# Adapter norm moved into a scan chain, split q/k/v projections, and paired max jobs in a four-layer conditioned sequence kernel

## The reference

```python
# layer 0: state-space layer with a complex scan, then an MLP 256 -> 1024 -> 256
y = y + gate_a * s5(ln(y) * (1 + scale_a) + shift_a)
y = y + gate_ff * (gelu(mod(ln(y)) @ W1 + b1) @ W2 + b2)
# layer 1: one-head attention over 1024 tokens, width 256
h = film(rmsnorm(x, norm1_w), cond, film1_w, film1_b)
Q = h @ q_w + q_b
K = h @ k_w + k_b
V = h @ v_w + v_b
attn = softmax(Q K^T * 256 ** -0.5)
x = x + ((attn @ V) @ proj_w + proj_b)
x = x + gelu(film(rmsnorm(x, norm2_w), ...) @ mlp_w1 + mlp_b1) @ mlp_w2 + mlp_b2
# layer 2: rank-8 adapter whose four maps are made from the conditioning row
h = gelu(layernorm(ada_emb, ln_g, ln_b) @ W1 + b1)
w = h @ W2 + b2
# layer 3: 16-head attention (head width 16) over 1024 tokens
energy = q k^T
att = softmax(energy) / 256 ** 0.5
```

## Time and profile before

| what | value |
|---|---|
| median of three runs | 879.32 us (878.69 to 881.57) |
| the profiled execution, its own time | 880.76 us |
| its span | 878.9 us |
| mean granted TensorE clock | 0.982 |
| PE busy | 838.7 us, 95% of the span |
| DVE busy | 666.1 us, 76% |
| ACT busy | 459.4 us, 52% |
| POOL busy | 227.3 us, 26% |

### The profile page before, as it was taken

The page is one execution under the profiler, slowest core; times in us unless marked ns, Lnnn a source line. Parts: engine busy times, 40 slices in busy tenths (PEclk is TensorE's granted clock), DMA queues, the critical chain, the costliest instruction groups (busy, mean ns, idle before and its releaser), DMA issues.

```text
span 878.9 us, 13287 instructions
## 1 busy us (share of the span) xinstructions
PE 838.7 (95%) x4978; PEld 521.8 (59%) x4978; DVE 666.1 (76%) x1139; ACT 459.4 (52%) x840; POOL 227.3 (26%) x377
## 2 busy tenths in 40 slices
PE   6999999999999999999989989999999999999994
PEld 3668888958977998887845433333333333333342
DVE  8998657676538577646458879999999999999377
ACT  4646232144332443333232158888878878888760
POOL 4443412202002103112112710233333333333411
PEclk9999999999999999999989969999999999999998
DMA  8613122110000000000597600505050505000002
GB/s 314 252 49 97 55 92 98 49 52 2 1 1 1 1 1 1 2 1 1 168 182 193 252 1 3 92 21 92 21 93 21 92 21 93 23 27 24 27 25 73
DMA packets 29379, 57.40 MB, mean 65 GB/s; under 512 B 7228, under 2 KB 15152, under 8 KB 29314
## 3 DMA queue, kind: packets, MB, share of 16 engines
q1 hardware_dynamic: 22596, 44.40, 19.2%
q0 software_dynamic: 6720, 12.15, 4.7%
HBM read 39.26 MB, written 14.91 MB: 62 GB/s over the span
## 4 chain that ended last, share of the span: by engine, by line
PE 83%; DVE 8%; ACT 5%; POOL 2%; issue 2%; DMA 0%; DVEq 0%; ACTq 0%; POOLq 0%
PE PA L1531 15%; PE PA L1542 15%; PE PD L1327 10%; PE PA L1305 8%; PE PA L1253 7%; PE PD L1502 7%; PE PA L1408 5%; PE PD L1378 4%; PE PA L1246 2%; PE PA L1398 1%; PE PD L1600 1%; DVE NMX L2045 1%; PE PA L1477 1%; ACT R L1107 1%; PE PD L1253 1%
## 5 line engine op out<-in xcount | busy, mean ns | idle before, releaser
L2045 DVE TENSOR_REDUCE NMX<-PD 128x2 f32<-128x1024 f32 x256 | 301.9, 1220 | 25.7 <-PE PD L1502 21.2
L1107 ACT ACTIVATE R<-PA 128x512 f32<-128x512 f32 x512 | 267.0, 603 | 71.6 <-PE PA L1531 69.8
L1531 PE MATMUL PA<-STKR 50*128 50x512 f32 x512 | 185.3, 454 | 3.6 <-ACT R L1107 2.5
L1531 PEld LDWEIGHTS PA<-STKR 50*128 50x128 f32 x512 | 83.2, 188 | 151.7 <-ACT R L1107 139.3
L1502 PE MATMUL PD<-STKR 48*128 48x512 f32 x512 | 150.0, 456 | 4.2 <-DVE NMX L2045 4.1
L1043 ACT ACTIVATE R<-PA,VEC 128x512 f32<-128x512 f32 x64 | 43.8, 687 | 104.1 <-PE PA L1305 91.6
L1327 PE MATMUL PD<-WHR,HSR 128*128 128x256 f32 x512 | 95.3, 285 | 0.5 <-DVE HSR L1918 0.5
L1327 PEld LDWEIGHTS PD<-WHR,HSR 128*128 128x128 f32 x512 | 82.1, 191 | 6.1 <-issue 2.0
L1305 PE MATMUL PA<-XSR,WHR 128*128 128x512 f32 x256 | 81.2, 398 | 3.9 <-issue 2.0
L1502 PEld LDWEIGHTS PD<-STKR 48*128 48x128 f32 x512 | 62.0, 188 | 30.1 <-DVE NMX L2045 13.4
L1327 PE MATMUL PD<-WLR,HSR 128*128 128x256 f32 x256 | 72.4, 283 | 0.0
(11 more groups left out here) (288 smaller groups left out, 1181.3 us busy)
## 6 DMA issues: line engine op xcount, KB each, us to landing
STKR<-qk_terms SPq DMA_DIRECT2D x32, 384.0 KB, 8.8
R<-in_l_w SPq DMA_DIRECT2D x8, 1024.0 KB, 5.0
W<-in_w SPq DMA_DIRECT2D x4, 1024.0 KB, 10.7
qk_terms<-PARTS SPq DMA_DIRECT2D x8, 512.0 KB, 3.4
qk_terms<-PARTS POOLq DMA_DIRECT2D x8, 512.0 KB, 3.8
S<-row_reciprocals POOLq DMA_DIRECT2D x56, 64.0 KB, 2.1
X<-in_x SPq DMA_DIRECT2D x4, 512.0 KB, 8.5
qk_terms<-PARTS SPq DMA_DIRECT2D x8, 256.0 KB, 5.0
```

The lines of the kernel that those rows point to most:

```text
L1107: act.activation(PB[:, n % 2, j, :], PA[:, e % NEB, :], ACT.Exp).then_inc(s_exp3, 1)
L1531: pe.matmul(PA[:, e % NEB, :], KS[rows, slot(gg), jj, kt * P:(kt + 1) * P], QS[rows, slot(gg), jj, c * HALF:(c + 1) * HALF], start=True, s ...
L2045: ve.tensor_reduce(out, PD[:, o:o + NROW, :], axis=AX_X, op=ALU.max, negate=True).then_inc(s_mred, 1)
```

## The change

Three edits of one file. (1) `ada_normalise` is called from `bu` of the second part, between the scan and the product with C2; the stage `an` is gone and `gc` moves ahead of `ad 0`. (2) The q, k and v projections of layer 1 use fp32r halves and three products: DVE splits the q and k weights in a new stage `wh`, the v weight in `wv`, and every XT tile in the DVE part of `n1`; the halves of the tiles lie where the MLP's halves lay (XSR), those of the weights in C2, S2 and in the place of WA. The stage `n1 0` moves three down jobs ahead, into the MLP. The last statistics and the norm of batch 1 leave the end of the MLP and run on DVE inside batch 0's attention, as jobs `hs` and `hn` behind the first and the second score of the loop. (3) In the 8 `qk3` jobs of batch 1 three max jobs come in twos; three fewer stand alone ahead of the first step, and the turn `tm` comes later by two max jobs.

```diff
-         ("an", 0), ("nn", 1), ("ya", 0), ("n0", 1), ("ad", 0), ("gc", 0), ("cg", 1), ("y0", 0), ("yn", 0), ("ad", 1), ("bu", 2),
+         ("nn", 1), ("ya", 0), ("n0", 1), ("gc", 0), ("ad", 0), ("cg", 1), ("y0", 0), ("yn", 0), ("ad", 1), ("bu", 2),
...
-             {NTILE - 1: [("h0", 0)], B * NTILE - 6: [("wt", 0)], B * NTILE - 4: [("wv", 0)]})
+             {NTILE - 1: [("h0", 0)], B * NTILE - 6: [("wt", 0)], B * NTILE - 5: [("wh", 0)], B * NTILE - 4: [("wv", 0)],
+              B * NTILE - 3: [("n1", 0)]})
...
-SCHED += weave([("qk3", QJOBS + j) for j in range(QJOBS - 1)], [("mx", EARLY + j) for j in range(QJOBS - 1)])
-EARLY += QJOBS - 1
-assert UNIT == EARLY
-SCHED += [("qk3", 2 * QJOBS - 1), ("mx", EARLY), ("tm", 0)]
-SCHED += weave([("v3", TWO + j) for j in range(TWO)], [("mx", EARLY + 1 + j) for j in range(TWO)])
-SCHED += [("mx", n) for n in range(EARLY + 1 + TWO, LEAD)]
+for j in range(QJOBS):
+    SCHED += [("qk3", QJOBS + j), ("mx", EARLY)]
+    EARLY += 1
+    if EARLY >= UNIT + 2 and ("tm", 0) not in SCHED:
+        SCHED.append(("tm", 0))
+    elif j % 2 and j < QJOBS - 1:
+        SCHED.append(("mx", EARLY))
+        EARLY += 1
...
+            jobs += [(("hs", "hn")[t], 0)] if t < 2 else []
...
             def qk(b):
+                pe.wait_ge(s_whalf, 2)
+                terms = [(k, w, x) for k in range(KB) for w, x in TERMS]
+                for name, weights in zip("qk", WQKV):
                     for c in range(NC):
-                        xt_ready(b, "n1", c)
+                        pe.wait_ge(s_half1, (b * NC + c + 1) * KB)
                         for k in range(KB):
-                            project(abank(b, name, c, k), WA[:, w], k * P, b, c, s_afull)
+                            o = abank(b, name, c, k)
+                            for n, (i, w, x) in enumerate(terms):
+                                m = pe.matmul(o, weights[w][:, i, k * P:(k + 1) * P],
+                                              XTR[:, (1 - b, b)[x], i, c * HALF:(c + 1) * HALF],
+                                              start=(n == 0), stop=(n == len(terms) - 1))
+                            m.then_inc(s_afull, 1)
...
+                if part == 1:
+                    ada_normalise(0)
                 ve.wait_ge(s_z, part + 1)
                 ve.tensor_tensor(ZC[:, q], Z[:, q], C2[:, q], ALU.mult).then_inc(s_zc, 1)
...
-                    if t % TPC == TPC - 1:
+                    if t % TPC == TPC - 1 and (b, h) != (B - 1, NC - 1):
                         stats(b, lambda h: None, [h])
...
+            def weight_halves(_):
+                ve.wait_ge(s_wain, 32)
+                for w in range(2):
+                    high, low = WQKV[w]
+                    link(ve.tensor_copy(high, WA[:, w]))
+                    ve.tensor_tensor(low, WA[:, w], high.bitcast(F32), ALU.subtract).then_inc(s_whalf, 1)
+
+            def tile_halves(b):
+                for _, tag, h, k in turned(b, "n1"):
+                    evacuated(ve, b, tag, h, k)
+                    high, low = (XTR[:, x, k, h * HALF:(h + 1) * HALF] for x in (1 - b, b))
+                    tile = XT[:, b, k, h * HALF:(h + 1) * HALF]
+                    link(ve.tensor_copy(high, tile))
+                    ve.tensor_tensor(low, tile, high.bitcast(F32), ALU.subtract).then_inc(s_half1, 1)
```

More of the change, by code:

```diff
@@ L133 @@
 SOLO = turn_step(NUNIT - 1) + 1
-SCHED += weave([("qk3", QJOBS + j) for j in range(QJOBS - 1)], [("mx", EARLY + j) for j in range(QJOBS - 1)])
-EARLY += QJOBS - 1
-assert UNIT == EARLY
-SCHED += [("qk3", 2 * QJOBS - 1), ("mx", EARLY), ("tm", 0)]
-SCHED += weave([("v3", TWO + j) for j in range(TWO)], [("mx", EARLY + 1 + j) for j in range(TWO)])
-SCHED += [("mx", n) for n in range(EARLY + 1 + TWO, LEAD)]
+for j in range(QJOBS):
[6 more added lines that the diff above has]
+        EARLY += 1
+assert ("tm", 0) in SCHED
+SCHED += weave([("v3", TWO + j) for j in range(TWO)], [("mx", EARLY + j) for j in range(TWO)])
+SCHED += [("mx", n) for n in range(EARLY + TWO, LEAD)]
 AFTER = {SOLO + 2 * j + i: [(("p3a", "p3")[i], j)] for j in range(TWO - 1) for i in range(2)}
@@ L193, in act_jobs @@
         for kind, x in attention(stage):
-            jobs += {"s": [], "v": [(b, "v1", x)], "t": [(b, "p", x, i) for i in range(2)], "o": [(b, "o", x)]}[kind]
+            jobs += {"s": [], "v": [(b, "v1", x)], "t": [(b, "p", x, i) for i in range(2)], "o": [(b, "o", x)]}.get(kind, [])
         return jobs
@@ L302, in build @@
             PARTS = [at(f"PARTS{u}", o, [P, 2, 2, HALF]) for u, o in enumerate((XN0, WA0))]
+            WAR = at("WAR", WA0, [P, 4, KB, D])
+            C2R = at("C2R", C20, [P, T])
+            S2R = at("S2R", C20 + T, [P, T])
             NMT = at("NMT", C20, [UNIT, NPART, P])
@@ L403, in build @@
         PX = R[:, 4096:6144].rearrange("p (s n) -> p s n", s=2)
+        XTR = XSR[:, :].rearrange("p (b k t) -> p b k t", b=B, k=KB)
+        WQKV = [[a.rearrange("p (k n) -> p k n", k=KB), WAR[:, w]]
+                for w, a in enumerate((C2R[:, KB * D:T], S2R[:, KB * D:T], C2R[:, 0:KB * D]))]
         WVT = C2[:, 0:KB * D].rearrange("p (k n) -> p k n", k=KB)
@@ L499, in build @@
         s_zs = sem("states_sin_ready")
+        s_half1 = sem("second_layer_tile_halves_ready")
+        s_whalf = sem("attention_weight_halves_ready")
         s_rowbias = sem("v_bias_in_rows")
@@ L1385, in values @@
                 o = abank(b, "v1", j)
+                terms = [(k, w, x) for k in range(KB) for w, x in TERMS]
                 for u in range(2):
                     t = 2 * j + u
-                    for k in range(KB):
-                        m = pe.matmul(o[:, u * D:(u + 1) * D], XT[:, b, k, t * P:(t + 1) * P], WA[:, 2, k, :],
-                                      start=(k == 0), stop=(k == KB - 1))
+                    for n, (k, w, x) in enumerate(terms):
+                        m = pe.matmul(o[:, u * D:(u + 1) * D], XTR[:, (1 - b, b)[x], k, t * P:(t + 1) * P], WQKV[2][w][:, k, :],
+                                      start=(n == 0), stop=(n == len(terms) - 1))
                 m.then_inc(s_afull, 1)
@@ L1938, in h0, with other_stats, other_normalise @@
             def h0(b):
-                normalise("h0", b, False)
+                if b == 0:
+                    normalise("h0", b, False)
+            def other_stats(b, _):
+                if b == 0:
+                    stats(B - 1, lambda h: None, [NC - 1])
+            def other_normalise(b, _):
+                if b == 0:
+                    normalise("h0", B - 1, False)
             def bank_of(*job):
@@ L1951, in wv @@
             def wv(b):
-                ve.tensor_copy(WA[:, 2].rearrange("p k d -> p (k d)"), bank_of(b, "wv", 0)).then_inc(s_aevd, 1)
+                high, low = (a.rearrange("p k n -> p (k n)") for a in WQKV[2])
+                o = bank_of(b, "wv", 0)
+                link(ve.tensor_copy(high, o))
+                ve.tensor_tensor(low, o, high.bitcast(F32), ALU.subtract).then_inc(s_aevd, 1)
                 row = BC[:, BP, :]
```

13 lines of the change are left out of this document (7 added, 6 removed).

## The result

| | before | changed |
|---|---|---|
| median of the first runs, us | 879.83 (878.69 to 881.57, 4 runs) | 873.81 (873.03 to 874.39, 4 runs) |
| a second group of runs | 881.57 (878.86 to 884.70, 11 runs) | 872.78 (870.37 to 875.78, 6 runs) |
| profiled execution, us | 880.76, span 878.9 | 873.36, span 871.5 |
| mean granted clock | 0.982 | 0.986 |

The ratio is 0.992 with a 95% interval from 0.9901 to 0.9939, in the second group 0.9897 (0.9874 to 0.9919). The forecast was 872.2 by a gain of 7.1; measured are 6.0 in the medians, 7.4 between the two profiled executions and 8.8 in the second group. The sum of what was worked out holds to 0.4 us in the trace; beside it stand four items of about 1 to 2 us each that were not in it.

What follows compares the result with a forecast made beforehand. PE was taken as the bound, busy 95% of the span; -3.0 - 0.2 - 0.9 + 1.5 - 2.75 + 0 - 1.7 = -7.05, say -7.1, from the median 879.32 gives 872.2 us. The range goes from 867.0 to 875.8.

Steps and rivals of the forecast that it cites:

- Projections: Layer 1's q and k projections: 48 fp32r products at 0.228 replace 32 float32 instructions; gains 3.0 (batch 0), 2.75 (batch 1).
- Turn ahead, and K's banks: Before batch 0's projections: the earlier turn gains 0.2; K's banks waiting for Q's first low half taken as 0, up to 1.
- Rest of V, batch 0: Batch 0's remaining V products: 5.18 us become 4.3 in 36 fp32r products, 0.9 gained.
- The norm in the attention: Batch 1's norm on DVE in batch 0's attention meets POOL's bias tiles; PE waits, 1.5 lost, bounds 0 and 5.5.
- Rival A: Batch 1's norm in batch 0's attention: DVE gets ahead of POOL, PE waits nowhere; gain 8.6, 870.7 us; chance 0.15.
- rival D: Same norm: its operations and POOL's bias tiles alternate without overlap, PE waits 3.5; gain 5.1, 874.2 us; chance 0.09.
- Batch 1's V: Batch 1's V products: DVE works nearly without a gap there, so faster V gives 0; bound 0.9.
- Adapter row: At the scans: PE's 1.49 idle goes, but it then waits for the hidden row; 0, bounds -0.9 and +0.3.
- Twos: Batch 1's qk jobs: three of five lone max jobs move between projections; 1.7 gained, bounds -2.3 and 0.
- The clock: Behind the lone max jobs: PE's clock still at 0.5 for about 13 us, as before; no term in the sum.
- the case that it does not fall at all: First steps: a shorter thin stretch keeps the clock full, three steps gain 1.2 each; 868.6 us; chance 0.20.
- The rival that ends slower: Batch 1's norm at its bound: PE idles 5.5, the halved clock costs 6.4; 882.6 us; 0.04 shared with another rival.

Runs made afterwards that it cites:

- e7: Changed kernel with batch 1's closing norm and statistics back behind the MLP's last block; median 878.03 us, ratio 0.9978 to the kernel before.
- e2: Changed kernel with batch 1's norm in two halves, behind the fourth and fifth turned tile, past POOL's bias tiles; median 870.75 us, ratio 0.9873 to before.
- e3: Changed kernel with POOL's eight bias tiles started only when batch 1's norm is done; median 871.05 us, ratio 0.9881 to the kernel before.
- e11: Changed kernel with twelve of batch 1's 96 products for V issued twice, as additional PE work; 873.55 us in one run.
- e4: Changed kernel without the twos, so five lone max jobs as before; median 875.22 us, ratio 0.9933 to the kernel before.
- e6: Kernel before with the max jobs in twos alone; median 878.05 us, ratio 0.9971 to the kernel before.
- e1: The changed kernel again, unedited, as yardstick of the second group; median 872.78 us, ratio 0.9897 to the kernel before.
- e9: Changed kernel with PE's idle time ahead of the first steps filled more fully by repeated max jobs and energies; median 870.90 us, ratio 0.9885 to before.
- e5: Kernel before with the adapter row's edit alone; median 879.62 us, ratio 0.9986 to the kernel before.

## Why the prediction was right, and where not

- **Projections.** -3.0 and -2.75 forecast, -2.97 and -2.82 measured. In batch 0, 2.79 of it are the projections themselves and 0.18 the way past the first V job. The price of 0.228 for a product, taken from the MLP's up jobs in the same form, held.
- **Turn ahead, and K's banks.** -0.2 and 0 forecast, -0.23 and +0.25 measured, the latter inside the -2.97. Q's lows began at 182.67, forecast 182.6. e7 shows how thin the cover was: 1.8 of statistics and the norm behind it brought a wait of 5.11.
- **Rest of V, batch 0.** -0.9 forecast, -0.70 measured; the products gave 0.87, and 0.17 went in the scores ahead of them (5.73 for 5.57).
- **The norm in the attention.** +1.5 forecast: an idle of 1.4, PE ready at 215.1, which is the 218.9 of the forecast less 3.8; measured 1.34 of idle and +1.60 up to batch 1's projections. The size is partly luck: by the working's own 0.5 per tile, 7.4 tiles beside the norm make 2.2 + 3.7, so it would have ended near 220.1 and PE waited 1.9, where the forecast has 219.6 and 1.4. Measured are 3.35 lost over eight tiles, 0.42 each. Rival A (hides) and rival D are out by the trace, and e2 and e3 show that the cause was the meeting. The Trainium skill ("SBUF — State Buffer", section "SBUF: two separate sides") has a GpSimd operation and a VectorE operation in a two-port mode, or one with two SBUF inputs, fully block each other for whole instructions. If the norm is such a case, whole turns would make 2.19 + 5.61 = 7.8 by the lone times of e3. Together they were done in 6.1 (209.65 to 215.79), POOL slowed by 7% and DVE to two and a half times: the measurement decides, and it says that DVE pays nearly all of it, and that either part overlaps or part of a lone time needs no turn; no row tells which.
- **Batch 1's V.** 0 forecast, 0 measured, and e11, a single run, bears out that the stretch is DVE's.
- **Adapter row.** 0 forecast, with -0.9 and +0.3 as bounds; -0.12 measured, -0.18 alone.
- **Twos.** -1.7 forecast, -1.44 measured up to the last max job. PE's wait at the turn was 0.71 (forecast 0.6). e4 and e6 give the same 1.43 to 1.45, with the rest of the change and without it.
- **The clock.** This is the step of the forecast that failed. The forecast's last part expected "still about 13 us at clock 0.5" behind the lone jobs and gave a change only to the case that it does not fall at all. It fell, for 7 us: the stretch 508.7 to 522.4 became 502.5 to 509.3, worth -1.94, and e6 shows the same 1.94. The fall near 447 in the kernel before was not looked at (-1.48), nor was the last projection as a place where the clock can fall (+1.40). With the late read (+0.90) these came to -1.1 in the profiled pair. So the forecast's terms gave -6.7, and that the total of -7.1 lies so near the measured -7.4 is luck in part: the items outside it, -3.4 and +2.3, nearly cancelled.

The rival that ends slower was far off: PE idled 1.34 and not 5.5. What stays open is why a low stretch lasts 3.4, 7, 10 or 14 us: five lone jobs go with the longer ones and two with the shorter, but the same steps followed in e1 (7) and e2 (10), and no run here varied only the moment of the fall.

## What to carry to other kernels

Before a DVE sequence is moved into a gap, look at what POOL runs there: 2.2 us of work became 5.5, and either a later place or a POOL queue that waits for the sequence gave 1.4 back. A move that gives nothing in the old order can be what another edit lives on: price it in the new order, with the queue that now stands behind it. Around any stretch where PE mostly waits, look at the granted clock behind it, give the slow steps a term of their own (in e7 they added 1.6 to a wait of 5.1), and try whether filling the stretch with repeated work is cheaper.

## What the runs showed of the hardware

- Eight DVE operations (128x256, one SBUF operand, float32) took 2.19 alone and 5.54 beside eight POOL additions of the same size, which took 5.99 for 5.61.
- Behind two windows in which PE was busy 0.68 and 0.54 of 2 us the granted clock was at its lower level; with the same stretch filled it stayed whole (e9). A step at the lower level took 3.8 to 4.1 for 2.6 to 2.8. The low stretch ahead of the first steps was 14, 14 and 10 us long in the three traces with five lone max jobs, and 7 us in six and 10 in one of the seven with two. Behind an idle of 5.11 in e7 it was 3.4 us, and 24 products took 7.11 for 5.47.
- One read of 8 KB from DRAM took 3.5 and 3.7 us in two of the traces, and PE lost 0.9 by it in the first. Of the 14 such reads at least one took 2.6 to 3.9 in each of ten traces of the changed kernel and its variants; the longest of the kernel before, e5 and e6 took 2.2.
- The wait for the first weights varied from 1.0 to 2.9 us (at 9 to 11 us of the span), a spread of 1.8, more than most of the effects that were measured.
